# Output projection of a retention layer: heads projected by fp32r parts with the weights stationary, transposed back per group

## What is computed

```
h = _layernorm(x, axis=-1) * (1 + ca) + sa
...
scores = scores * decay[None]
o = jnp.einsum('bhts,bhsv->bhtv', scores, v)
...
o = (o - mean) * jax.lax.rsqrt(var + EPS)
o = o * gn_weight.reshape(H, V) + gn_bias.reshape(H, V)
o = o.reshape(Bx, Tx, H * V)
o = o * jax.nn.silu(g)
return jnp.einsum('btc,oc->bto', o, Wo)
...
x = x + ga * _L0_attn_ref(h, ...)
h = _layernorm(x, axis=-1) * (1 + cb) + sb
x = x + gb * _L0_ffn_ref(h, ...)
```

## Time and profile before

| | before |
|---|---|
| median of 3 runs | 767.81 us (767.59 to 768.0) |
| the profiled execution | 768.16 us |
| its span, first to last instruction | 766.4 us |
| mean granted TensorE clock | 0.984 |
| busy: PE, DVE, POOL, ACT | 737.5, 606.3, 587.1, 452.4 us |
| chain that ended last: PE, DVE | 86%, 8% |
| products `outs<-wo_gated,y` | 992 instructions, 131.3 us busy |

### The profile page before, as it was taken

One profiled execution on the slowest core, in us unless ns is written; L12 is line 12 of the kernel. 1 busy time (PEld: TensorE's weight loads), 2 busy tenths in 40 slices (PEclk: granted clock), 3 DMA queues, 4 the chain that ended last, 5 costly groups with the idle time before them and its releaser, 6 DMA issues.

```text
span 766.4 us, 29026 instructions
## 1 busy us (share of the span) xinstructions
PE 737.5 (96%) x12093; PEld 649.7 (85%) x12093; DVE 606.3 (79%) x1283; ACT 452.4 (59%) x819; POOL 587.1 (77%) x641
## 2 busy tenths in 40 slices
PE   5788999999999999999999999999999999999996
PEld 3577888888988888888888888888888888888875
DVE  6978777888878788887878878797887878786545
ACT  4234555656565565656556565656656565656664
POOL 3746787897878888798878987788887987777641
PEclk9889999999999999999999999999999999999998
DMA  9422211121223132122313212231321222122100
GB/s 327 123 51 50 44 39 38 41 43 34 47 51 71 23 72 49 40 55 43 71 30 71 43 30 65 50 70 24 71 45 35 65 43 57 23 58 43 37 15 29
DMA packets 66402, 42.46 MB, mean 55 GB/s; under 512 B 38232, under 2 KB 55904, under 8 KB 66272
## 3 DMA queue, kind: packets, MB, share of 16 engines
q1 hardware_dynamic: 65552, 39.81, 22.3%
q10 hardware_dynamic: 720, 0.80, 0.3%
HBM read 11.22 MB, written 4.20 MB: 20 GB/s over the span
## 4 chain that ended last, share of the span: by engine, by line
PE 86%; DVE 8%; issue 3%; ACT 1%; POOL 1%; DMA 1%; ACTq 0%; DVEq 0%; POOLq 0%
PE ring L280 48%; PE O_E L280 14%; PE outs L280 13%; PE ring L295 7%; PE O_O L280 3%; DVE N L916 1%; PE ring L319 1%; DVE gn_sum L909 1%; DVE h_full L845 1%; DVE turned L860 1%; DVE swapped L865 1%; DMA wmod<-in_w_mod 1%; ACT N L619 1%; DVE sin_k L882 1%; DVE rot_k L879 1%
## 5 line engine op out<-in xcount | busy, mean ns | idle before, releaser
L1145 POOL TENSOR_TENSOR y<-y,gate 128x512 f32<-128x512 f32 x123 | 155.1, 1282 | 24.7 <-ACT y L631 24.7
L280 PEld LDWEIGHTS outs<-wo_gated,y 128*128 128x128 f32 x992 | 127.7, 191 | 10.2 <-POOL y L1145 1.7
L1128 POOL TENSOR_TENSOR rot_k<-rot_k,sin_k 128x256 f32<-128x256 f32 x128 | 108.5, 868 | 34.1 <-DVE sin_k L882 34.1
L280 PE MATMUL outs<-wo_gated,y 128*128 128x128 f32 x992 | 131.3, 275 | 1.1 <-POOL y L1145 1.0
L909 DVE TENSOR_REDUCE gn_sum<-N 128x4 f32<-128x512 f32 x128 | 81.9, 681 | 48.6 <-ACT N L619 48.5
L1138 POOL TENSOR_TENSOR gn_rstd<-gn_var,minus_half 128x8 f32<-128x8 f32 x64 | 105.4, 1646 | 5.0
L1122 POOL TENSOR_TENSOR qT<-qT,swapped 128x512 f32<-128x512 f32 x64 | 83.2, 1300 | 19.8 <-DVE swapped L865 19.6
L631 ACT ACTIVATE y<-ring,gn 128x512 f32<-128x512 f32 x126 | 91.0, 777 | 4.8 <-PE ring L295 4.8
L600 ACT ACTIVATE v_odd<-ring 128x512 f32<-128x512 f32 x64 | 38.4, 599 | 92.2 <-PE ring L280 92.2
L889 DVE TENSOR_TENSOR A<-ring,consts 128x256 f32<-128x256 f32 x128 | 48.0, 417 | 50.9 <-PE ring L280 50.9
L903 DVE TENSOR_TENSOR S<-ring,S 128x512 f32<-128x512 f32 x112 | 76.9, 686 | 1.9
(11 more groups left out here) (149 smaller groups left out, 2101.9 us busy)
## 6 DMA issues: line engine op xcount, KB each, us to landing
v<-v_odd SPq DMA_DIRECT2D x128, 128.0 KB, 2.3
k_odd<-rot_k SPq DMA_DIRECT2D x128, 64.0 KB, 2.2
X<-in_x SPq DMA_DIRECT2D x16, 256.0 KB, 3.4
out<-X SPq DMA_DIRECT2D x15, 256.0 KB, 3.2
key_tables<-in_const SPq DMA_DIRECT2D x7, 256.0 KB, 8.3
rotary_q<-in_const_q SPq DMA_DIRECT2D x2, 512.0 KB, 8.3
gates<-stored_rows SPq DMA_DIRECT2D x8, 128.0 KB, 3.2
N<-in_w_qkT SPq DMA_DIRECT2D x1, 512.0 KB, 4.7
```

What stands on the lines that cost most here:

```text
L280: return e.matmul(o, lhsT, rhs, start=start, stop=stop, skip_group_check=True)
L1128: done = e.tensor_tensor(turned[:, n, :, :], turned[:, n, :, :], sin[:, n, :, :], op)
L1145: e.tensor_tensor(y[:, n % NY, :], y[:, n % NY, :], gate[:, n % 2, :], ALU.mult).then_inc(sem["y"])
```

## The change

`project_out` now holds the weights stationary: `wo` is split once into fp32r parts (`split_w_o`, on ACT and POOL), and a head is three matmuls of 512 columns, wo_hi*y_hi, wo_hi*y_lo, wo_lo*y_hi, into `outs`, which now has channels on the partitions. For that ACT rounds each gated head (`round_y`, `y_hi`) and DVE computes the rest (`low_y`, `y_lo`). Once a group ACT copies `outs` to `outT` with the gate `ga` as its per-partition scale (`gate_out`), and PE transposes it back in four instructions into a bank of `ring` (`turn_out`), from which DVE adds the residual. The gate products on POOL (`gate_weights`) and `wo_gated` go. `y` has two buffers in place of four, freed by `low_y`, and the parts two each. Both `project_out` of a step stand together, right behind `state` (and `project_r`). `residual` and the `norm_stats` that follow it move from step 4g + 8 to 4g + 9 and ahead of `rotate_k`; ACT's `norm_apply` for them moves to the start of step 4g + 9. The last two heads keep fp32 products, with weights that were gated beforehand (`last_wo`).

```
             def project_out(n):
                 g, h = divmod(n, H)
+                cols = slice(h * C, (h + 1) * C)
+                at.wait_ge("w_o_lo", 1)
+                at.wait_ge("y_hi", n + 1)
+                at.wait_ge("y_lo", n + 1)
                 if h == 0:
-                    at.wait_ge("residual", g)
-                at.wait_ge("wo_gated", 2 * (g // GB) + 1 + h // PAIRS)
-                at.wait_ge(*gated(n))
...
+                    at.wait_ge("out_T", g)
+                high, low = (y_parts[s][:, n % NYH, :] for s in ("hi", "lo"))
+                matmul(out_bank[:, :], wo["hi"][:, cols], high, h == 0, False)
+                matmul(out_bank[:, :], wo["hi"][:, cols], low, False, False)
+                matmul(out_bank[:, :], wo["lo"][:, cols], high, False, n % H == H - 1 or n == LAST_HEADS[0] - 1
+                       ).then_inc(sem["out_head"])
+
+            def turn_out(g):
+                bank = take_bank(("out", g), ("residual", g + 1))
+                at.wait_ge("out_T", g + 1)
                 for j in range(GC):
-                    done = matmul(outs(g)[j], y[:, n % NY, j * P:(j + 1) * P], wo_gated[:, h, :],
-                                  h == 0 and j in (0, PJ if g == LAST else 0), h == H - 1)
-                done.then_inc(sem["out_head"])
+                    done = e.transpose(bank[:, j * P:(j + 1) * P], outT[:, j * P:(j + 1) * P], ident)
+                done.then_inc(sem["out_back"])
...
@@ PE's steps
-                for i in due(step - 6, 1, NCHUNK - 1):
-                    project_out(2 * i + 1)
...
                 for g in due(step - 13, GC, LAST - 1):
                     project_r(g)
+                for i in due(step - 6, 1, NCHUNK - 1):
+                    project_out(2 * i)
+                for i in due(step - 6, 1, NCHUNK - 1):
+                    project_out(2 * i + 1)
...
-                for i in due(step - 5, 1, NCHUNK - 1):
-                    project_out(2 * i)
+                for g in due(step - 9, GC, LAST):
+                    turn_out(g)
...
+            def round_y(n):
+                at.wait_ge(*gated(n))
+                at.wait_ge("out_head", n - NYH + 1)
+                e.activation(y_parts["hi"][:, n % NYH, :], y[:, n % NY, :], ACT.Copy).then_inc(sem["y_hi"])
+
+            def gate_out(g):
+                at.wait_ge("out_head", LAST_HEADS[0] if g == LAST else H * (g + 1))
+                at.wait_ge("gate_cols", 1)
+                at.wait_ge("out_back", g)
+                e.activation(outT[:, :], out_bank[:, :], ACT.Identity, bias=nought[:, :], scale=gate_cols[:, g // GB:g // GB + 1]
+                             ).then_inc(sem["out_T"])
...
@@ ACT's steps
+                for g in due(step - 8, GC, NGROUP):
+                    gate_out(g)
+                for g in due(step - 9, GC, LAST):
+                    norm_apply(g, 1)
...
+                for i in due(step - 4, 1, NCHUNK - 1):
+                    round_y(2 * i)
+                for i in due(step - 4, 1, NCHUNK - 1):
+                    round_y(2 * i + 1)
...
-                for g in due(step - 8, GC, LAST):
-                    norm_apply(g, 1)
...
             def residual(g):
                 xg = X[:, g % NX, :, :]
-                at.wait_ge("out_head", H * (g + 1))
-                e.tensor_tensor(xg, xg, by(GC, out_bank[:, :]), ALU.add).then_inc(sem["residual"])
+                at.wait_ge("out_back", g + 1)
+                e.tensor_tensor(xg, xg, by(GC, bank_of["out", g][:, :]), ALU.add).then_inc(sem["residual"])
+
+            def low_y(n):
+                at.wait_ge("y_hi", n + 1)
+                e.tensor_tensor(y_parts["lo"][:, n % NYH, :], y[:, n % NY, :], y_parts["hi"][:, n % NYH, :].bitcast(F32), ALU.subtract
+                                ).then_inc(sem["y_lo"])
...
@@ DVE's steps, behind norm_heads
+                for g in due(step - 9, GC, LAST):
+                    residual(g)
+                for g in due(step - 9, GC, LAST):
+                    norm_stats(g, 1)
+                for i in due(step - 5, 1, NCHUNK - 1):
+                    low_y(2 * i)
+                for i in due(step - 5, 1, NCHUNK - 1):
+                    low_y(2 * i + 1)
                 for i in due(step + 2, 1, NCHUNK):
                     rotate_k(i)
-                for g in due(step - 8, GC, LAST):
-                    residual(g)
-                for g in due(step - 8, GC, LAST):
-                    norm_stats(g, 1)
```

More of the change, by code:

```diff
@@ L56 @@
+    "w_qk_hi", "w_qk_lo", "w_v", "w_v_centred", "w_v_hi", "w_v_lo", "wffn_v", "x0", "x1", "x2", "x3", "x4", "x5",
+    "x6", "y", "y_hi", "y_lo",
 )
@@ L448, in last_out @@
                     for j in range(GC)[chunks_of(part)]:
[L449 removed]
+                        done = matmul(last_outs(j), y[:, n % NY, j * P:(j + 1) * P], last_wo[:, n % 2, :],
                                       False, n == LAST_HEADS[1])
@@ L537, in _ @@
                     project_gate(2 * i + 1)
-                for _ in due(step, 1, 1):
+                for _ in due(step - 1, 1, 1):
                     mod_gates()
@@ L723, in _ @@
                     split_w_v()
+                for _ in due(step - 1, 1, 1):
+                    split_w_o()
                 for i in due(step, 1, NCHUNK):
@@ L1025, in _ @@
             for step in steps:
-                for b in due(step - 6, CB, B):
+                for b in due(step - 10, CB, B):
                     ffn_weights(b)
@@ L1029, in _ @@
                     norm_stats(g, 0)
-                for i in due(step - 6, 1, NCHUNK - 1, NCHUNK - GC):
-                    last_gate(2 * i + 1)
                 for g in due(step - 11, GC, LAST):
@@ L1045, in _ @@
                     rotate_q(m)
-                for _ in due(step, 1, 1):
+                for i in due(step - 5, 1, NCHUNK - 1, NCHUNK - GC):
+                    last_gate(2 * i + 1)
+                for _ in due(step - 1, 1, 1):
                     mod_gates()
@@ L1183, in _ @@
                     mix_delta(g)
-                for g in due(step - 7, GC, LAST):
-                    norm_rstd(g, 1)
                 for g in due(step - 11, GC, LAST - 1):
```

187 lines of the change are left out of this document (108 added, 79 removed).

## The result

The changed kernel takes 932.4 us (931.4 to 934.4, four runs) against 767.7 (765.8 to 768.0) for the kernel before: a ratio of 1.216, 95% interval 1.213 to 1.218. The direction and the mechanism of the forecast held; the time lies above its range (822 to 925). The profiled run took 931.4 us.

What follows compares the result with a forecast made beforehand. PE, busy 737.5 of 766.4 us, was taken as the bound. 766.4 + 66 (later `sin_k` in the loop) + 51 (clock falls) + 1 (program end) = 884.4 us of span, forecast as 886; range 822 to 925.

Steps and rivals of the forecast that it cites:

- The bound and the mechanism: In the loop PE waits for `sin_k` at the key transposes in two steps of four, 2.6 to 3.0 us each.
- r2: Loop steps with remainder 2 modulo 4, such as step 34: 13.4 us forecast, from 10.76, before falls of the clock.
- The subtraction, 0.70 us: On DVE ahead of `rotate_k`: each of two subtractions a chunk adds 0.70 us, so `sin_k` is 1.4 us later.
- r3: Loop steps with remainder 3 modulo 4, such as step 35: 23.9 us forecast together with r0, from 22.10.
- r0: Loop steps with remainder 0 modulo 4, such as step 36: 23.9 us forecast together with r3, from 22.10.
- r1: Loop steps with remainder 1 modulo 4, such as step 37: no wait of PE, 12.2 us forecast, from 12.07.
- The clock, 51 us: Half clock behind PE's waits slows attention, scores and recall: 1.8 us twice a group, +51 us.
- The tail, +1: End of the program: `gate_out` and `last_turn_out` ahead of the last two heads, eight fp32 instructions, +1 us.
- PE's own part, -1.0 a group: On PE: products -1.56 us a group, transposes back and change of type +0.55; PE alone would win 1.0.
- The clock holds: Rival: everything as forecast but without falls of PE's clock, 835 us; chance 0.17.
- Only ACT's chain counts: Rival: key bank free in time, ACT's two more copies delay scores, +1.4 us a group net, 788 us; chance 0.10.
- All subtractions collide with POOL and falls stretch r1: Rival: DVE's subtractions take 0.90 us each, clock falls add 1.7 us a group, 933 us; chance 0.11.

Runs made afterwards that it cites:

- the waits filled: Changed kernel with PE's waits filled by repeated key products and repeated transposes of the normalised heads, nothing left out: 887.4 us, ratio 1.157.
- the one on the kernel before: Kernel before with only two unused SBUF subtractions more a step on DVE, ahead of each key rotation: 858.3 us, ratio 1.117.
- with the products first as well: Changed kernel without rounding of y in the loop, both heads' products moved to the start of PE's step: 772.7 us, ratio 1.009.

## Why the prediction was too low

**The bound and the mechanism: right.** PE waits for `sin_k`; DVE is 76% busy and no engine is full; in r2 DVE waits for `y_hi`; the clock falls behind the waits: 28 falls begin in the loop, where the forecast had 28.5, though some last 6.8 us and not 3.4 (123 us at half clock in all). The runs with the subtractions behind the rotation (80 us), with the copies moved (30), with the waits filled (45) and the one on the kernel before (90 lost) show the links apart.

**The subtraction, 0.70 us: the step that failed.** From the first `gn_sum` of a step, averages of the trace in us:

| | r2 | r3 | r0 | r1 |
|---|---|---|---|---|
| both subtractions, forecast | 1.40 | 1.40 | 1.40 | 1.40 |
| measured | 2.00 | 2.27 | 1.78 | 1.26 |
| end of `sin_k`, forecast | 9.9 | 9.6 | 8.2 | 11.3 |
| measured | 10.80 | 10.41 | 8.89 | 11.27 |
| step, forecast with the falls | 15.2 | 25.7 with r0 | | 12.2 |
| measured | 16.09 | 26.83 with r0 | | 12.14 |

A group: 55.1 instead of 53.1, or 28 of the 30 us by which the loop missed. The prediction chose 0.70 "since in three of the four steps POOL has by then finished" its query rotation. For r2 that was true of the old order only. The delay that moves `normed` by 1.4 moves `h2T` and with it POOL: its query rotation ended 6.86 after `gn_sum` before, and 8.46 after (averages):

```profile
428.09 1.04 POOL L1230 TENSOR_TENSOR delta<-h2T 128x512 f32<-128x512 f32 x1 [1.06 <-ACT h2T L692]
429.09 1.26 POOL L1198 TENSOR_TENSOR qT<-qT,swapped 128x512 f32<-128x512 f32 x1
```

The rotation now runs from 429.09 to 430.35, beside the pair of 429.48. For r3 and r0 the old order itself already showed the collision, had POOL been read there. POOL's lines of one group before, in r2, r3 and r0:

```profile
404.68 1.29 POOL L1122 TENSOR_TENSOR qT<-qT,swapped 128x512 f32<-128x512 f32 x1
416.45 1.27 POOL L1107 TENSOR_TENSOR hT_lo<-h_full,hT_hi 128x512 fp32r<-128x512 f32 x1 [0.68 <-ACT hT_hi L593]
427.24 1.28 POOL L1122 TENSOR_TENSOR qT<-qT,swapped 128x512 f32<-128x512 f32 x1
```

In r3 POOL works on the low part of `hT` from 6.5 to 7.8 after `gn_sum`, in r0 on the queries from 6.2 to 7.5, and the subtractions were to stand where the key rotation began, at 6.2 and 5.5. The size was misjudged in kind as well. One subtraction of the pair keeps its 0.68 us, and the one that meets POOL takes 1.37 to 1.42 in r2 and 1.75 to 1.78 in r3 (and in r0 in 5 steps of 12), far above the 0.90 taken as upper bound. Only r1, which the prediction took to be the bad case, had both at their short time (1.26 for two).

Not all of the 2.0 us a group is this. In r2 `sin_k` was 0.90 late, and the run with POOL's query rotation late gave 0.63 of that back; in r3 and r0 the excess of the pair is 0.87 and 0.38, and one of the two counts. That makes about 1.25 us a group, or 18 of the 28 us, as an estimate; the rest was not traced.

**The clock, 51 us: right.** At least 46 by the filled waits. The row at 430 shows the fall behind waits of 2.06 and 1.53 us in a row. It begins 0.10 us after PE resumed there and 0.34 after it at 459.81, where the prediction took some 0.5. By the Trainium skill (TensorE: Matmul & The Clock Gate, Why this matters for your kernels) the clock would have held through most of these waits; the measurement decides. The forecast's "mean near 0.85" was a slip: its own 28 falls of 3.4 us and the old 24 us give 0.93; it is 0.919. Of the 930 us 151 were at 1.2 GHz, 126 more than before, and something over a third of these (46) is lost time; the rest cost nothing that the runs show. The length of a wait alone does not tell whether the clock falls. In the kernel before with two subtractions, PE resumed at 261.93 after 2.71 us and at 365.44 after 2.70, and the clock was 0.62 behind the one and 1.00 behind the other:

```profile
262.00:270.00 8.00, 8.00 (x143) 0.62 0.01 2
366.00:374.00 8.00, 8.00 (x153) 1.00 0.17 37
```

With the subtractions behind the rotation a single wait of 2.08 us, at 295.66, left it at 1.00 (296 to 304).

**The tail, +1: wrong, +15.2.** The prediction counted PE's instructions in it and not the chain. In the end of the program nothing hides the new links, as in this piece of the chain that ended last (start, length, what):

```profile
884.42 1.39 PE outs L287 x6
...
888.57 0.70 DVE X L986
...
896.20 1.07 ACT gate L660 x2
897.27 0.53 ACT y_hi L673
897.82 0.70 DVE y_lo L990
...
898.66 2.90 PE outs L287 x6
...
904.61 0.63 ACT y_hi L673
905.26 1.29 DVE y_lo L990 x2
```

The tail is 79 to 82 us in every run with the subtractions and with both products behind the state products, 70.9 without the subtractions, 70.8 without any rounding and 67.9 with the products first as well. So nine of the 15 are the subtractions', three the place of the products, and three what is left; the copies are worth nothing here once the subtractions are gone. PE's products in this chain are dearer as well where they stand behind a wait: the six at 898.66 ran at half clock. With this term right the forecast would have been 900, and with the 28 us of the loop too 928.

**PE's own part, -1.0 a group: its size right by half, its effect wrong.** PE has 0.56 us less to do in a group, and nothing of it arrives. The products themselves were priced rightly, 0.23 us each (468.63, 468.87, 469.10 above; the 131 ns of the Trainium skill, TensorE: Matmul & The Clock Gate, Back-to-back issue gap, is nowhere near). What was not priced is the cover that they gave: it is worth 20 us of loop. In the sum this stood inside the wait of r2 (transposes due at 6.9), so it didn't falsify the total.

**The rivals.** "The clock holds" gave 835; it did not hold. "Only ACT's chain counts" gave 788 and is what the run without subtractions tests: 815.5. Of the excess of 27, 19 are the loop, with the wait for `v`, which no part of the prediction had, and with the missing cover of the products; 5 are the tail and 2 the start. "All subtractions collide with POOL and falls stretch r1" gave 933, the measured time, and that was luck, for its reason was half right: they collide, but in r2, r3 and r0, and r1 has no fall (12.2 forecast without one, 12.14 measured). It had 24 us for falls that stretch r1 among others, and nothing for the 15 of the tail.

**The range** does not follow from its own words: 835 less 9 is 826, and 886 plus half of the 47 us of the last rival is 910, where 822 and 925 were given.

## What to carry to other kernels

Idle time of an engine is of use only in the place where it lies: DVE was idle for 20% before, four fifths of it behind the instruction on which PE waited (78 of 98 us over the steps 12 to 60), and two subtractions a step ahead of that instruction cost 117 us, behind it 37. When a product is moved on the bounding engine, ask what it covered where it stood. And a delay found on one engine has to be carried to every other before the contention between two of them is judged; then look for the serial chain at the end of the program, where each new link counts in full.

## What the runs showed of the hardware

- A DVE subtraction of two SBUF operands of 128x512 takes 0.66 to 0.70 us while POOL stands still. One that begins while a POOL operation on SBUF operands of 128x256 or 128x512 is running takes as long as that one still needs, and 0.55 more: the changed kernel has 31 subtractions of more than 1 us, 1.37 to 1.78 us long, and every one began beside such an operation and ended 0.545 to 0.551 us after it. Over the eleven runs that have `y_lo` there are 420, at 0.544 to 0.553. So it is held up, not slowed. In r1 the subtraction was there first: it kept its 0.65 to 0.69 us, and POOL's small `ln_var` and `ln_neg`, which take 0.20 and 0.23 us elsewhere, took 0.56 and 0.66.
- DVE's products with one operand in PSUM, `sin_k` and those of the queries, took 675 to 688 ns as a mean in every run, beside POOL or not. The Trainium skill (SBUF — State Buffer, Who interferes with whom) says so: two SBUF inputs contend with a POOL instruction that reads SBUF, one does not. The trace agrees, and adds the price.
- The granted clock fell towards its lower level of 1.2 GHz behind waits of PE of 3.07 us, and of 2.06 and 1.53 in a row, and not behind one of 0.82. One of 2.70 us and one of 2.08 left it at 1.00, each in another run, so the length of one wait does not decide. Repeated work in the place of the waits kept it at 0.99 in the loop, and made the kernel faster though PE had more to do.
